# One-core recommender kernel: the last four single transfers become two paired ones, and the end pieces wait for less

## The chip, the cores and the metric

The kernel runs on one core of a Trainium2 chip. The metric is the device time of one execution in microseconds (us). Three runs of the kernel before the change took 133.70, 133.76 and 133.83 us; the median is 133.76 us.

## The reference, cut to what matters

The input is a matrix of 1024 rows (the batch) by 12500 columns in 32-bit floats, about 51 MB, and everything else is small. What is computed:

```python
x_reg = input_data @ W_lin.T + b_lin                       # 12500 -> 1
emb = input_data @ factors                                 # 12500 -> 16
sum_squared = jnp.square(emb.sum(axis=1))
squared_sum = (jnp.square(input_data) @ jnp.square(factors)).sum(axis=1)
h = jax.nn.relu(emb @ W1.T + b1)                           # 16 -> 128
h = jax.nn.relu(h @ W2.T + b2)                             # 128 -> 64
x = x_reg + 0.5 * (sum_squared - squared_sum)[:, None] + h @ W3.T + b3
x = 0.5 + jax.nn.sigmoid(x) * 5.0
```

Every element of the input is used twice by TensorE: once as it is (against 17 columns: the 16 factors and the linear weight) and once squared.

## The kernel before, in words

The input comes transposed, so that the 12500 dimensions lie on the partitions in chunks of 128. A first chunk and a remainder of 84 dimensions are loaded for all 1024 batch columns. The other 96 chunks are worked on in groups of eight (`CHUNKS`), each group for one half (512 columns) of the batch, so a group is 128 partitions x 8 x 512 floats, 2 MB, with 16 KB for each partition. Groups 0 to 11 are the first batch half. Groups 12 to 19 are the first 64 chunks of the second half (`TOTAL` is 20). The last 32 chunks of the second half, the end, come in nine smaller `PIECES`: four of the block of 352 columns, five of the block of 160.

All loads are issued from one queue, SyncE's (L263 to L290), in program order. The buffer `xr` has six slots of one group each. A load into a slot waits on the semaphore `sq_used` until the group that used the slot last has been multiplied: TensorE raises `sq_used` by one behind the last matmul of a group's squares, starting from `RING` = 3, so a value of 3 + n says that n groups are done. Groups 0 to 15 (`PAIRED`) are loaded two at a time, by one transfer of 4 MB with 32 KB for each partition (L268 to L274). Groups 16 to 19 are loaded one at a time, by transfers of 2 MB with 16 KB for each partition (L275 to L278), each with a semaphore of its own. The end pieces lie in slots 2 to 5 of `xr`, and piece i waits for `sq_used` to reach `RING + TOTAL - SLOTS + END_SLOT + last_slot(i) + 1` (L283), where `END_SLOT` is 2 and `last_slot(i)` is 0 to 3 for slots 2 to 5. In numbers: pieces 0 and 1 wait until group 17 is done, pieces 2 and 3 until group 18 is done, pieces 4 to 8 until group 19 is done.

What each engine does with a group: VectorE squares three of its eight chunks (L424 to L428), ScalarE squares five (L324 to L328), GpSimd copies its weights to a ring of three (`place`, L304 to L309), and TensorE multiplies the eight chunks (`multiply`) and then the eight squared chunks (`add_squares`), with 16 matmul instructions each. The eight chunks go to the four 32-column quarters of the array in turn. For a pair (`pair`) TensorE's order is: wait for the pair's landing, multiply both groups, then the squares of both. For a single group it is: wait for the group's landing, multiply it, then its squares. The squares go to a ring of three groups in `sq`.

Behind group 11 the dense layers of batch block 0 run (from 76 to 81 us in the profile). The end has an order written out by hand on TensorE, VectorE and ScalarE: `multiply_end(i)` and its squares for pieces 0 to 3, then pieces 4 to 8 mixed with the dense layers of block 1, and then the dense layers of block 2 (`first_layer`, `layer2`, `layer3`, a sigmoid and a scaling), the store and the end. The squares of pieces 0 to 3 are written over the `sq` ring, and for this `square_end` of piece 0 also waits until group 18 has been multiplied, and that of piece 2 until group 19 has.

Of the kernel before, what the change touches and what calls it, by code (L numbers as in the profile page):

```python
# [14 lines left out]
P = 128  # L15
# [4 lines left out]

REST = N % P
HALF = B // 2
CHUNKS = 8
# [5 lines left out]
GROUPS = (ALL - 1) // CHUNKS  # L32
END_GROUPS = ENDS // CHUNKS
TOTAL = 2 * GROUPS - END_GROUPS
PAIRED = 16
W_END = ALL - ENDS

END_SLOT = TOTAL % SLOTS
# [10 lines left out]

PITCH = CHUNKS * HALF + 64
PAIR_PITCH = TWO * CHUNKS * HALF + 64


# [27 lines left out]
HD = HD_L + REST_SETS * LIN  # L83


def fm_kernel(nc, head, x_first, x_rest, x_pairs, x_groups, x_end, out):
    with ExitStack() as ctx:
        def sb(name, shape, dt=F32):
            return ctx.enter_context(nc.sbuf_tensor(name, shape, dt))
# [4 lines left out]
        def sem(name):  # L94
            return ctx.enter_context(nc.semaphore(name))
# [38 lines left out]
        first_landed = sem("first_landed")  # L134
        rest_landed = sem("rest_landed")
        x_landed = [sem(f"x_landed{t}") for t in range(SLOTS // TWO)]
        single_landed = [sem(f"single_landed{g}") for g in range(PAIRED, TOTAL)]
        end_landed = [sem(f"end_landed{i}") for i in range(len(PIECES))]
        y_stored = sem("y_stored")
        zero_set = sem("zero_set")  # L140
# [91 lines left out]

            engine.wait_ge(x_landed[s // TWO], 16 * (r + 1))

        def single(engine, g):
            engine.wait_ge(single_landed[g - PAIRED], 16)

        def chunks(i):
            return sum(PIECES[i][2]) + sum(PIECES[i][3])

        def last_slot(i):
            k, c = PIECES[i][:2]
            return (ENDS * (BLOCKS[k][0] - HALF) + (c + chunks(i)) * BLOCKS[k][1] - 1) // (CHUNKS * HALF)
# [19 lines left out]
        @block.sync  # L263
        def _(sp):
            sp.dma_start(hd[:, :], head).then_inc(hd_landed, 16)  # L265
            sp.dma_start(xf[:, :], x_first).then_inc(first_landed, 16)  # L266
            sp.dma_start(xl[:, :, :].rearrange("p c b -> p (c b)"), x_rest).then_inc(rest_landed, 16)  # L267
            for p in range(PAIRED // TWO):  # L268
                at = TWO * p % SLOTS
                if TWO * p >= SLOTS:  # L270

                    sp.wait_ge(sq_used, RING + TWO * p + TWO - SLOTS)
                sp.dma_start(xr[:, at:at + TWO].rearrange("p s c b -> p (s c b)"),  # L273
                             x_pairs[p, :, 0:TWO * CHUNKS * HALF]).then_inc(x_landed[at // TWO], 16)  # L274
            for g in range(PAIRED, TOTAL):  # L275
                sp.wait_ge(sq_used, RING + g + 1 - SLOTS)
                sp.dma_start(xr[:, g % SLOTS].rearrange("p c b -> p (c b)"),
                             x_groups[g - PAIRED, :, 0:CHUNKS * HALF]).then_inc(single_landed[g - PAIRED], 16)  # L278
            at = 0
            for i in range(len(PIECES)):  # L280
                c, n = PIECES[i][1], chunks(i)
                rows = x_end[at:at + P * n * width(i)].rearrange("(p m) -> p m", p=P)
                sp.wait_ge(sq_used, RING + TOTAL - SLOTS + END_SLOT + last_slot(i) + 1)  # L283
                sp.dma_start(piece(i, c, n), rows).then_inc(end_landed[i], 16)
                at += P * n * width(i)

            for k in range(len(BLOCKS)):
                sp.wait_ge(y_ready[k], 1)
                sp.dma_start(out[cols(k)].rearrange("(q b) -> q b", q=4), y[0:P:32, line(k)]).then_inc(y_stored, 16)
            sp.wait_ge(y_stored, 16 * len(BLOCKS))  # L290
# [26 lines left out]
        @block.scalar  # L317
        def _(act):
            act.wait_ge(zero_set, 1)
            nc.scalar.activation(warm[:, :], zero[:, 0:1], ACT.Sigmoid)  # L320
            act.wait_ge(first_landed, 16)
            nc.scalar.activation(sqf[:, :], xf[:, :], ACT.Square).then_inc(first_squared, 1)  # L322

            def squares(r, s):  # L324

                act.wait_ge(sq_used, SLOTS * r + s + 1)
                nc.scalar.activation(sq[:, ring(s), BY_DVE:CHUNKS, :], xr[:, s, BY_DVE:CHUNKS, :],  # L327
                                     ACT.Square).then_inc(act_squared, 1)  # L328

            def square_end(i, j=0):  # L330
                c = PIECES[i][1] + sum(PIECES[i][2][:j])
                n = PIECES[i][2][j]
                if j == 0:
                    act.wait_ge(end_landed[i], 16)
                    if frees_more(i):
                        act.wait_ge(sq_used, squares_free(i))
                nc.scalar.activation(squared_piece(i, c, n), piece(i, c, n),  # L337
                                     ACT.Square).then_inc(act_end_squared, 1)

            def copy_lin(k, u):  # L340
                nc.scalar.copy(lin[:, part(k, u)], p_lin[k][:, u * BLOCKS[k][1] // 2:(u + 1) * BLOCKS[k][1] // 2]  # L341
                               ).then_inc(lin_ready[k], 1)

            def layer1(k, n):
                act.wait_ge(p_h1_done[k], 1)
                c = BLOCKS[k][0]
                nc.scalar.activation(h1[:, c:c + n], p_h1[0][:, 0:n], ACT.Relu,
                                     bias=pr[:, C_B1:C_B1 + 1]).then_inc(h1a_ready[k], 1)

            def embedding_square(k):  # L350
                act.wait_ge(p_es_done[k], 1)
                nc.scalar.activation(gsq[:, line(k)], tot_bank(k)[:, line(k)], ACT.Square).then_inc(gsq_ready[k], 1)

            def sigmoid(k):
                act.wait_ge(p_tot_done[k], 1)
                nc.scalar.activation(sg[:, line(k)], tot_bank(k)[:, line(k)], ACT.Sigmoid,
                                     bias=bias[:, :]).then_inc(sg_ready[k], 1)

            with act.Fori(0, GROUPS // SLOTS) as r:
                for s in range(SLOTS):  # L360
                    landed(act, r, s)
                    squares(r, s)

            act.wait_ge(sq_used, RING + GROUPS)
            copy_lin(0, 0)
            copy_lin(0, 1)
            layer1(0, BLOCKS[0][1] // 2)
            embedding_square(0)
            act.wait_ge(bias_ready, 1)
            sigmoid(0)  # L370

            for g in range(GROUPS, PAIRED):
                landed(act, g // SLOTS, g % SLOTS)
                squares(g // SLOTS, g % SLOTS)
            for g in range(PAIRED, TOTAL):
                single(act, g)
                squares(g // SLOTS, g % SLOTS)

            square_end(0, 0)
            square_end(0, 1)  # L380
            square_end(1, 0)
            square_end(1, 1)
            square_end(2)
            square_end(3)
            square_end(4, 0)
            act.wait_ge(p_lin_done[1], 1)
            copy_lin(1, 0)
            copy_lin(1, 1)
            nc.scalar.copy(rest[:, :], p_lin[1][:, BLOCKS[1][1]:HALF]).then_inc(rest_copied, 1)
            embedding_square(1)  # L390
            square_end(4, 1)
            layer1(1, BLOCKS[1][1])
            square_end(5, 0)
            square_end(5, 1)
            square_end(6, 0)
            square_end(6, 1)
            square_end(7, 0)
            square_end(7, 1)
            square_end(8)
            sigmoid(1)  # L400
            embedding_square(2)
            act.wait_ge(squares_done, 1)
            nc.scalar.copy(qs[:, :], p_sq[:, 0:BLOCKS[LAST][1]]).then_inc(qs_ready, 1)
            sigmoid(2)

        @block.vector
        def _(dve):
# [16 lines left out]
            def squares(r, s):  # L424

                dve.wait_ge(sq_used, SLOTS * r + s + 1)
                nc.vector.tensor_tensor(sq[:, ring(s), 0:BY_DVE, :], xr[:, s, 0:BY_DVE, :], xr[:, s, 0:BY_DVE, :],  # L427
                                        ALU.mult).then_inc(dve_squared, 1)  # L428
# [40 lines left out]
            layer2(0)  # L469
            scale(0)  # L470

            for g in range(GROUPS, PAIRED):
                landed(dve, g // SLOTS, g % SLOTS)
                squares(g // SLOTS, g % SLOTS)
            for g in range(PAIRED, TOTAL):
                single(dve, g)
                squares(g // SLOTS, g % SLOTS)

            square_end(0, 0)
# [24 lines left out]
        def _(pe):  # L504
# [40 lines left out]
            def multiply(r, s, h):  # L545
                pe.wait_ge(wr_ready, SLOTS * r + s + 1)
                for c in range(CHUNKS):
                    add_mm(quad(p_lin[h], c, LIN, 0, HALF), wr[:, ring(s), c, :], xr[:, s, c, :])
# [108 lines left out]
            embedding_square(0)  # L657
            layer3(0)

            for g in range(GROUPS, PAIRED, TWO):  # L660
                pair(g // SLOTS, g % SLOTS, 1)
            for g in range(PAIRED, TOTAL):
                single(pe, g)
                multiply(g // SLOTS, g % SLOTS, 1)
                add_squares(g // SLOTS, g % SLOTS, 1)

            pe.wait_ge(ws_ready, 2)
            for i in range(3):
# [102 lines left out]
```

## Time and profile before

| | |
|---|---|
| median of 3 runs | 133.76 us |
| the profiled execution | 133.76 us |
| its span in the profile | 132.0 us |
| mean granted TensorE clock | 0.974 |
| TensorE busy (matmul) | 107.0 us, 81% of the span |
| ScalarE, VectorE, GpSimd busy | 61.5, 52.6, 15.7 us |
| loaded from HBM | 52.2 MB, 396 GB/s over the span |

The span is the stretch from the first to the last record of the profile; 1.76 us of the execution's time lie around it. The chip's queues of transfers are busy nearly throughout. PE is TensorE, PEld its weight loads, SPq the queue of SyncE, which does nothing here but issue transfers. A granted clock of 1.00 is 2.4 GHz, one of 0.50 is 1.2 GHz.

### The profile page before, as it was taken

The numbers are of one execution on the slowest core, as the hardware profiler recorded it, in microseconds if no ns is written. First come the engines' busy times: TensorE is split into PE (matmuls) and PEld (weight loads), VectorE is DVE, ScalarE is ACT, GpSimd is POOL, SyncE is SP. The second block draws the span as 40 slices with busy tenths as digits, with TensorE's granted clock in tenths as the row PEclk, the third lists the DMA queues.
The fourth block names the chain that finished last, engine by engine and source line by source line (L and its number), as shares of the span: only waits on it lengthen the run. The fifth ranks groups of instructions, "written<-read, shape, count | busy, mean of one in ns | idle before, by whom it ended". The sixth has DMA issues, their size and how long they took to land.

```text
span 132.0 us, 2607 instructions
## 1 busy us (share of the span) xinstructions
PE 107.0 (81%) x1123; PEld 34.6 (26%) x1123; DVE 52.6 (40%) x51; ACT 61.5 (47%) x52; POOL 15.7 (12%) x48
## 2 busy tenths in 40 slices
PE   6099969429979839749749979999998987989992
PEld 4012222002212112112112233322222112345881
DVE  0391063027036036046045016565351351576571
ACT  4030067029039039049048046868562561465851
POOL 3015000200010200200200110164530000000000
PEclk9999999995999999999977999999999999999999
DMA  3999899989999998998999999899999999999700
GB/s 106 413 531 417 377 477 472 407 387 467 427 387 462 457 427 387 457 437 387 467 457 427 387 457 447 377 432 412 452 407 407 462 415 417 418 404 411 302 26 1
DMA packets 3489, 52.36 MB, mean 397 GB/s; under 512 B 404, under 2 KB 536, under 8 KB 1560
## 3 DMA queue, kind: packets, MB, share of 16 engines
q1 hardware_dynamic: 3480, 52.23, 93.2%
q8 instruction: 7, 0.11, 0.4%
q14 instruction: 2, 0.02, 0.0%
HBM read 52.22 MB, written 0.00 MB: 396 GB/s over the span
## 4 chain that ended last, share of the span: by engine, by line
DMA 54%; PE 40%; SPq 2%; DVE 1%; issue 1%; ACT 1%
DMA xr<-in_x_pairs 43%; PE p_lin L506 34%; DMA xr<-in_x_end 11%; PE p_sq L506 2%; PE p_h L601 2%; SPq L273 1%; PE p_tot L506 1%; PE p_h L632 1%; PE p_tot L614 0%; DVE h L454 0%; DVE h L449 0%; SPq L267 0%; SPq L266 0%; PE p_tot L621 0%; SPq L265 0%
## 5 line engine op out<-in xcount | busy, mean ns | idle before, releaser
L327 ACT ACTIVATE sq<-xr 128x2560 f32<-128x2560 f32 x20 | 45.9, 2333 | 46.8 <-DMA xr<-in_x_pairs 38.8
L427 DVE TENSOR_TENSOR sq<-xr 128x1536 f32<-128x1536 f32 x20 | 34.6, 1761 | 53.7 <-DMA xr<-in_x_pairs 42.9
L506 PE MATMUL p_lin<-xr,wr 128*17 128x512 f32 x320 | 39.9, 638 | 15.6 <-DMA xr<-in_x_pairs 14.4
L506 PE MATMUL p_lin<-sq,wz 128*18 128x512 f32 x320 | 37.7, 592 | 0.0
L506 PEld LDWEIGHTS p_lin<-xr,wr 128*17 128x17 f32 x320 | 9.2, 102 | 44.5 <-issue 38.4
L307 POOL COPY wr<-hd 128x136 f32 (+1 forms) x20 | 9.3, 464 | 75.0 <-PE p_lin L506 75.0
L506 PEld LDWEIGHTS p_lin<-sq,wz 128*18 128x18 f32 x320 | 10.1, 98 | 25.8 <-issue 25.0
L506 PE MATMUL p_lin<-xr,hd 128*17 128x352 f32 (+1 forms) x128 | 10.0, 380 | 1.3 <-DMA xr<-in_x_end 1.3
L437 DVE TENSOR_TENSOR sq<-xr 128x1408 f32<-128x1408 f32 (+3 forms) x6 | 6.6, 1135 | 6.1 <-DMA xr<-in_x_end 6.1
L337 ACT ACTIVATE sq<-xr 128x1408 f32<-128x1408 f32 (+3 forms) x6 | 5.7, 983 | 6.3 <-DMA xr<-in_x_end 6.3
L506 PE MATMUL p_lin<-sq,ws 128*18 128x352 f32 x64 | 6.6, 459 | 0.0
L506 PE MATMUL p_lin<-xf,hd 128*17 128x512 f32 x4 | 3.6, 1046 | 3.4 <-DMA xf<-in_x_first 3.4
L506 PEld LDWEIGHTS p_lin<-xr,hd 128*17 128x17 f32 x128 | 4.3, 97 | 5.2 <-issue 3.3
L308 POOL COPY wz<-s_all 128x8 f32 (+1 forms) x20 | 5.5, 273 | 0.0
L437 DVE TENSOR_TENSOR xr<-xr 128x320 f32<-128x320 f32 (+1 forms) x9 | 3.7, 451 | 2.2 <-DMA xr<-in_x_end 2.1
L506 PE MATMUL p_sq<-xr,ws 128*18 128x160 f32 x64 | 4.0, 300 | 0.0
L337 ACT ACTIVATE xr<-xr 128x320 f32<-128x320 f32 (+1 forms) x9 | 3.4, 432 | 0.9 <-DMA xr<-in_x_end 0.8
L449 DVE TENSOR_SCALAR h<-p_h,hd 128x256 f32<-128x256 f32 (+1 forms) x2 | 0.9, 434 | 6.9 <-PE p_h L601 6.8
L410 DVE SCALAR_TENSOR_TENSOR fsq<-hd 128x1552 f32<-128x1552 f32 x1 | 1.8, 1774 | 4.4 <-DMA hd<-in_head 4.4
L322 ACT ACTIVATE sqf<-xf 128x1024 f32<-128x1024 f32 x1 | 1.1, 1057 | 4.6 <-DMA xf<-in_x_first 4.6
L341 ACT COPY lin<-p_lin 128x256 f32<-128x256 f32 (+1 forms) x4 | 1.2, 342 | 4.2 <-PE p_lin L506 4.1
L506 PEld LDWEIGHTS p_lin<-sq,ws 128*18 128x18 f32 x64 | 2.4, 97 | 2.4 <-issue 1.4
(52 smaller groups left out, 40.8 us busy)
## 6 DMA issues: line engine op xcount, KB each, us to landing
xr<-in_x_pairs SPq DMA_DIRECT2D x8, 4096.0 KB, 21.9
xr<-in_x_groups SPq DMA_DIRECT2D x4, 2048.0 KB, 18.3
xr<-in_x_end SPq DMA_DIRECT2D x1, 2112.0 KB, 10.5
xr<-in_x_end SPq DMA_DIRECT2D x3, 640.0 KB, 12.0
xr<-in_x_end SPq DMA_DIRECT2D x1, 1760.0 KB, 14.3
xr<-in_x_end SPq DMA_DIRECT2D x1, 1056.0 KB, 12.4
hd<-in_head SPq DMA_DIRECT2D x1, 952.0 KB, 4.8
xr<-in_x_end SPq DMA_DIRECT2D x1, 704.0 KB, 13.7
```

Source lines behind the costliest of these rows:

```text
L273: sp.dma_start(xr[:, at:at + TWO].rearrange("p s c b -> p (s c b)"), x_pairs[p, :, 0:TWO * CHUNKS * HALF]).then_inc(x_landed[at // TWO], 16)
L307: nc.gpsimd.tensor_copy(wr[:, ring(s), :, :], w[:, bass.ds(at, CHUNKS), :]).then_inc(wr_ready, 1)
L308: nc.gpsimd.tensor_copy(wz[:, ring(s), :, LIN:WZ].rearrange("p c k -> p (c k)"), s_all[:, bass.ds(at, CHUNKS)]).then_inc(wz_ready, 1)
L327: nc.scalar.activation(sq[:, ring(s), BY_DVE:CHUNKS, :], xr[:, s, BY_DVE:CHUNKS, :], ACT.Square).then_inc(act_squared, 1)
L337: nc.scalar.activation(squared_piece(i, c, n), piece(i, c, n), ACT.Square).then_inc(act_end_squared, 1)
L341: nc.scalar.copy(lin[:, part(k, u)], p_lin[k][:, u * BLOCKS[k][1] // 2:(u + 1) * BLOCKS[k][1] // 2]).then_inc(lin_ready[k], 1)
L410: nc.vector.scalar_tensor_tensor(fsq[:, :, :], w[:, :, 0:EMB], -0.5, w[:, :, 0:EMB], ALU.mult, ALU.mult).then_inc(fsq_ready, 1)
L427: nc.vector.tensor_tensor(sq[:, ring(s), 0:BY_DVE, :], xr[:, s, 0:BY_DVE, :], xr[:, s, 0:BY_DVE, :], ALU.mult).then_inc(dve_squared, 1)
L437: nc.vector.tensor_tensor(squared_piece(i, c, n), piece(i, c, n), piece(i, c, n), ALU.mult).then_inc(dve_end_squared, 1)
L506: return nc.tensor.matmul(out, lhsT, rhs, start=False, stop=False, skip_group_check=True)
L601: mm = nc.tensor.matmul(bank[32 * t:32 * t + 32, 0:n], pr[:, C_W1 + 32 * t:C_W1 + 32 * t + 32], rhs, start=True, stop=True, skip_group_che ...
L632: mm = nc.tensor.matmul(p_h2[32 * t:32 * t + 32, row(k)], pr[:, C_W2 + t % 2 * 32:C_W2 + t % 2 * 32 + 32], h1[:, part(k, t // 2)], start=T ...
```

## The change

All twenty groups are loaded in pairs, so that the last four come by two transfers of 4 MB with 32 KB for each partition. `PAIRED`, the tensor `x_groups`, the semaphores `single_landed` and the loops over singles on SyncE, ScalarE, VectorE and TensorE go. Groups 16 and 17 go into slots 4 and 5 when group 11 is done, groups 18 and 19 into slots 0 and 1 when group 13 is done. TensorE works on them with `pair`. And `END_SLOT` goes out of the condition of the end pieces, which therefore wait for two groups less: pieces 0 and 1 until group 15 is done, pieces 2 and 3 until group 16 is, pieces 4 to 8 until group 17 is.

```diff
-            for p in range(PAIRED // TWO):
+            for p in range(TOTAL // TWO):
                 at = TWO * p % SLOTS
                 if TWO * p >= SLOTS:
                     sp.wait_ge(sq_used, RING + TWO * p + TWO - SLOTS)
                 sp.dma_start(xr[:, at:at + TWO].rearrange("p s c b -> p (s c b)"),
                              x_pairs[p, :, 0:TWO * CHUNKS * HALF]).then_inc(x_landed[at // TWO], 16)
-            for g in range(PAIRED, TOTAL):
-                sp.wait_ge(sq_used, RING + g + 1 - SLOTS)
-                sp.dma_start(xr[:, g % SLOTS].rearrange("p c b -> p (c b)"),
-                             x_groups[g - PAIRED, :, 0:CHUNKS * HALF]).then_inc(single_landed[g - PAIRED], 16)
...
-                sp.wait_ge(sq_used, RING + TOTAL - SLOTS + END_SLOT + last_slot(i) + 1)
+                sp.wait_ge(sq_used, RING + TOTAL - SLOTS + last_slot(i) + 1)
...
-            for g in range(GROUPS, PAIRED):
+            for g in range(GROUPS, TOTAL):
                 landed(act, g // SLOTS, g % SLOTS)
                 squares(g // SLOTS, g % SLOTS)
-            for g in range(PAIRED, TOTAL):
-                single(act, g)
-                squares(g // SLOTS, g % SLOTS)
...
-            for g in range(GROUPS, PAIRED, TWO):
+            for g in range(GROUPS, TOTAL, TWO):
                 pair(g // SLOTS, g % SLOTS, 1)
-            for g in range(PAIRED, TOTAL):
-                single(pe, g)
-                multiply(g // SLOTS, g % SLOTS, 1)
-                add_squares(g // SLOTS, g % SLOTS, 1)
```

VectorE's loops change as ScalarE's do. On the host, the rows of groups 16 to 19 are laid out as those of the other pairs.

## Rows read from the trace of the kernel before

**Rows 1.** Page, slices of the span, and the chain that ended last.

```profile
DMA  3999899989999998998999999899999999999700
...
DMA 54%; PE 40%; SPq 2%; DVE 1%; issue 1%; ACT 1%
```

**Rows 2.** Chain in order of time: start us, us, what.

```profile
38.47 7.10 PE p_lin L506 x64
...
67.65 8.66 PE p_lin L506 x64
...
80.17 20.91 PE p_lin L506 x192
101.08 0.02 issue
101.09 0.33 SPq L284
101.42 0.04 issue
101.47 14.35 DMA xr<-in_x_end
115.82 0.04 issue
115.86 6.75 PE p_lin L506 x92
```

**Rows 3.** Timeline of ScalarE, squares of pairs and singles: start, us, [idle before <-releaser].

```profile
28.74 4.57 ACT L327 ACTIVATE sq<-xr 128x2560 f32<-128x2560 f32 x2 [6.62 <-DMA xr<-in_x_pairs]
...
86.98 4.57 ACT L327 ACTIVATE sq<-xr 128x2560 f32<-128x2560 f32 x2 [1.87 <-DMA xr<-in_x_pairs]
91.88 2.35 ACT L327 ACTIVATE sq<-xr 128x2560 f32<-128x2560 f32 x1 [0.33 <-DMA xr<-in_x_groups]
...
106.56 2.35 ACT L327 ACTIVATE sq<-xr 128x2560 f32<-128x2560 f32 x1 [2.55 <-DMA xr<-in_x_groups]
111.61 1.38 ACT L337 ACTIVATE sq<-xr 128x1408 f32<-128x1408 f32 x1 [2.71 <-DMA xr<-in_x_end]
```

**Rows 4.** Stages of the end: us, busy of PE, PEld, DVE, ACT, POOL, PEclk, DMA share, GB/s.

```profile
106.56:111.61 5.05, 4.27 (x32) 0.92 (x32) 1.76 (x1) 2.35 (x1) 0.00 (x0) 1.00 1.00 427
115.84:121.79 5.95, 5.93 (x81) 2.96 (x85) 4.30 (x5) 3.73 (x5) 0.00 (x0) 1.00 1.00 408
121.79:127.04 5.25, 5.25 (x158) 4.46 (x155) 3.55 (x10) 4.61 (x14) 0.00 (x0) 1.00 0.57 223
```

**Rows 5.** Timeline, weight loads of TensorE that show its pace, groups and end pieces.

```profile
81.27 0.12 PEld L506 LDWEIGHTS p_lin<-xr,wr 128*17 128x17 f32 x4 [0.31 <-issue]
81.70 0.12 PEld L506 LDWEIGHTS p_lin<-xr,wr 128*17 128x17 f32 x4 [0.31 <-issue]
...
112.02 0.13 PEld L506 LDWEIGHTS p_lin<-xr,hd 128*17 128x17 f32 x4 [0.17 <-issue]
112.32 0.13 PEld L506 LDWEIGHTS p_lin<-xr,hd 128*17 128x17 f32 x4 [0.16 <-issue]
```

**Rows 6.** Timeline of TensorE: after pairs; the last group; the end pieces.

```profile
57.94 1.05 PE L506 MATMUL p_lin<-xr,wr 128*17 128x512 f32 x8 [2.67 <-DMA xr<-in_x_pairs]
...
106.58 1.91 PE L506 MATMUL p_lin<-xr,wr 128*17 128x512 f32 x16 [0.63 <-DMA xr<-in_x_groups]
...
111.73 0.49 PE L506 MATMUL p_lin<-xr,hd 128*17 128x352 f32 x4 [0.87 <-DMA xr<-in_x_end]
...
115.86 1.66 PE L506 MATMUL p_lin<-xr,hd 128*17 128x352 f32 x18 [0.39 <-DMA xr<-in_x_end]
```

**Rows 7.** Timeline around the landings of pieces 4 and 6.

```profile
121.72 0.17 PEld L506 LDWEIGHTS p_lin<-xr,hd 128*17 128x17 f32 x6 [0.17 <-DMA xr<-in_x_end]
...
124.93 0.49 DVE L437 TENSOR_TENSOR xr<-xr 128x320 f32<-128x320 f32 x1 [0.74 <-DMA xr<-in_x_end]
124.94 0.55 PEld L506 LDWEIGHTS p_lin<-xr,hd 128*17 128x17 f32 x16
124.98 0.30 PE L506 MATMUL p_sq<-xr,ws 128*18 128x160 f32 x2
125.03 0.80 PE L506 MATMUL p_lin<-xr,hd 128*17 128x160 f32 x16
```

**Rows 8.** Granted clock by stretches of 2 us, columns as in rows 4.

```profile
68.00:70.00 2.00, 2.00 (x12) 0.35 (x8) 2.00 (x2) 2.00 (x2) 0.00 (x0) 0.50 0.80 344
```

More of the change, by code:

```diff
@@ L34 @@
 TOTAL = 2 * GROUPS - END_GROUPS
-PAIRED = 16
 W_END = ALL - ENDS
@@ L48 @@
 BY_DVE = 3
-PITCH = CHUNKS * HALF + 64
 PAIR_PITCH = TWO * CHUNKS * HALF + 64
@@ L83, with fm_kernel @@
 HD = HD_L + REST_SETS * LIN
-def fm_kernel(nc, head, x_first, x_rest, x_pairs, x_groups, x_end, out):
+def fm_kernel(nc, head, x_first, x_rest, x_pairs, x_end, out):
     with ExitStack() as ctx:
@@ L136, in fm_kernel @@
         x_landed = [sem(f"x_landed{t}") for t in range(SLOTS // TWO)]
-        single_landed = [sem(f"single_landed{g}") for g in range(PAIRED, TOTAL)]
         end_landed = [sem(f"end_landed{i}") for i in range(len(PIECES))]
@@ L233, in landed @@
             engine.wait_ge(x_landed[s // TWO], 16 * (r + 1))
-        def single(engine, g):
-            engine.wait_ge(single_landed[g - PAIRED], 16)
         def chunks(i):
@@ L470, in _ @@
             scale(0)
-            for g in range(GROUPS, PAIRED):
+            for g in range(GROUPS, TOTAL):
                 landed(dve, g // SLOTS, g % SLOTS)
-                squares(g // SLOTS, g % SLOTS)
-            for g in range(PAIRED, TOTAL):
-                single(dve, g)
                 squares(g // SLOTS, g % SLOTS)
@@ L658, in _ @@
             layer3(0)
-            for g in range(GROUPS, PAIRED, TWO):
+            for g in range(GROUPS, TOTAL, TWO):
                 pair(g // SLOTS, g % SLOTS, 1)
-            for g in range(PAIRED, TOTAL):
-                single(pe, g)
-                multiply(g // SLOTS, g % SLOTS, 1)
-                add_squares(g // SLOTS, g % SLOTS, 1)
             pe.wait_ge(ws_ready, 2)
@@ L729 @@
     chunks = xT[P + REST:].reshape(ALL - 1, P, B)
-    x_pairs = np.zeros((PAIRED // TWO, P, PAIR_PITCH), f32)
-    x_groups = np.zeros((TOTAL - PAIRED, P, PITCH), f32)
+    x_pairs = np.zeros((TOTAL // TWO, P, PAIR_PITCH), f32)
     for g in range(TOTAL):
         h, c = g // GROUPS, CHUNKS * (g % GROUPS)
-        rows = chunks[c:c + CHUNKS, :, h * HALF:(h + 1) * HALF].transpose(1, 0, 2).reshape(P, -1)
-        if g < PAIRED:
-            at = g % TWO * CHUNKS * HALF
-            x_pairs[g // TWO, :, at:at + CHUNKS * HALF] = rows
-        else:
-            x_groups[g - PAIRED, :, :CHUNKS * HALF] = rows
+        at = g % TWO * CHUNKS * HALF
+        x_pairs[g // TWO, :, at:at + CHUNKS * HALF] = chunks[c:c + CHUNKS, :, h * HALF:(h + 1) * HALF].transpose(1, 0, 2).reshape(P, -1)
     ends = chunks[ALL - 1 - ENDS:]
@@ L762 @@
     params[:, C_B3] = np.asarray(L0_rec_b3)
-    arrays = {"head": head, "x_first": x_first, "x_rest": x_rest, "x_pairs": x_pairs, "x_groups": x_groups, "x_end": x_end}
+    arrays = {"head": head, "x_first": x_first, "x_rest": x_rest, "x_pairs": x_pairs, "x_end": x_end}
     nc = bacc.Bacc("TRN2", target_bir_lowering=False, num_devices=1)
```

## The prediction

> **What bounds the kernel now.** I read the page's slices first, then the chain in order of time, then the starts of ScalarE's squares, then the end in stages. The slices show transfers busy at 8 or 9 tenths up to the last two microseconds of the load, and the chain gives them 54% of the span [rows 1]. So for the first hundred microseconds the stream of loads is the bound: a pair lands, the engines work it off, and they wait. From the landing at 28.74 us to that at 86.98 us six pairs arrive, so one takes 58.24/6 = 9.71 us [rows 3]. The four singles take from 86.98 to 106.56 us, 19.58 us, or 4.895 each [rows 3]. The first question is whether the stream has a hole that earlier issues could close. It has none: the last group lands at 106.56, the first end piece at 111.61, and between the two the transfers are busy at a share of 1.00 with 427 GB/s [rows 3, 4], though that piece was issued only at 101.09 [rows 2]. It was issued late, yet 5.5 us before the queue would have run dry (106.56 - 101.09).
>
> The end has another bound. The chain's last step that waits for a transfer ends at 115.82, with piece 1, and behind it stand matmuls [rows 2]. From 115.84 to 121.79 TensorE is busy for 5.93 of 5.95 us, and from there to 127.04, when the last block's first sums are read, for 5.25 of 5.25 [rows 4]. Busy time alone could be drawn-out waiting, so I check it by pace. A group's weight loads come four at a time every 0.43 us (81.27, 81.70), those of an end piece of 352 columns every 0.295 us (112.02 and 112.32 give 0.30; I use 0.295) [rows 5]. Pieces 1, 2 and 3 have 10 + 6 + 4 = 20 chunks, each with two matmuls as it is and two squared: 80, or 20 steps of 0.295 = 5.9 us. From 115.86 this ends at 121.76, and piece 4, which lands near 121.7, is waited for with 0.17 us of idle weight loading and no more [rows 7]. So TensorE works without a pause from piece 1 on, and the loads arrive just in time. The Trainium skill (Trainium Kernel Development and Optimization, Performance Expectations) warns that matmul busy time is a bad metric, since matmuls are pipelined. That rule speaks against reading the 5.93 us as a bound; the pace of the weight loads agrees with it being one in this stretch.
>
> **The change part by part.** *Issue conditions of the end pieces.* They fall by two groups. Pieces 0 and 1 are then issued near 94 us in place of 101.09. I cost this at nothing: what hides it is the 5.5 us of transfers still ahead of them in the queue. Were that cover gone in the changed kernel, it would be a loss, but the issue is earlier, never later, and the pair of groups 18 and 19 waits for group 13, as group 19 does now. Below nothing the bound is that the pieces would arrive at the pair's pace of 432 GB/s (4.19 MB in 9.71 us) in place of 408 [rows 3, 4] for their 8.4 MB, some 1.1 us on the stream. I take zero: the share is already 1.00, and TensorE isn't waiting for that stream anyway.
>
> *Rows of 32 KB.* Two pairs take 19.42 us in place of the 19.58 of four singles [rows 3]. The last pair lands at 86.98 + 19.42 = 106.40, so the stream is 0.16 us ahead. Its bounds are 0 (if the 0.16 is the scatter of the landings) and 0.16; I take 0.16. Two issues on SyncE go, which lie beside the transfers.
> The Trainium skill (DMA: Bandwidth & Descriptors, the anatomy of one DMA) gives each transfer a fixed 2.0 us beside its bytes; it is measured on another issue path. By that rule alone two transfers fewer would give back 4 us. The singles' spacing of 4.895 us for 2.10 MB, against 6.8 by the rule, disagrees: in a full queue the fixed part lies beside the previous transfer [rows 3].
>
> *Groups 18 and 19 arrive together.* This is the part that costs. Now group 18 lands one group ahead of 19 and is worked off in the meantime, and only group 19's work is left behind the last landing of a group at 106.56. With the pair, two groups' work lies behind it. A group is 32 matmuls, eight steps of 0.43 = 3.44 us [rows 5]; the pair is 6.88. (A pair at the full clock takes 7.10 in the chain, with the run-out of its last matmul [rows 2].) The squares don't hold it up: the second group's ScalarE squares are ready 4.57 us behind the landing [rows 3], and TensorE wants them after 3 x 1.72 + 0.65 = 5.8 us. Then comes piece 0: 12 chunks, 48 matmuls, 12 steps of 0.295 = 3.54 us. Its squares may begin once group 18 is done, 5.2 us plus run-out behind the landing, near 111.9; they take ScalarE and VectorE some 2.4 us and are wanted at 115.1, so they are hidden.
> TensorE starts the pair at 106.42, ends it at 113.30, ends piece 0 at 116.84, and only then comes to piece 1, which it now starts at 115.86 [rows 6]. That is 0.98 us later. The other way round: today TensorE sits idle for 0.87 us before piece 0 and 0.39 before piece 1 [rows 6], plus some 1.1 us of waiting for squares and run-outs inside 106.58 to 115.86 (9.28 us less 3.44, 3.54, 0.87 and 0.39 leaves 1.04), 2.30 in all; group 18 puts 3.44 in, 0.16 come back from the stream: 3.44 - 2.30 - 0.16 = 0.98.
>
> *What of this reaches the end.* From piece 1 on TensorE has no pause that could take it up, except the short waits for pieces 4 and 6: under 0.1 us each, 0.13 together as I read them (121.72 against 121.79, 124.93 against 124.98) [rows 7]. The dense layers of block 1 and 2, the squares and the copies hang on TensorE's steps in the same order and move with it. So 0.98 - 0.13 = +0.85 us. In the profiled execution 133.76 becomes 134.61; that execution is equal to the median of the runs, 133.76, and so the forecast for the median is 134.6. If the stream gains nothing it is 134.77; if the pauses are larger than I read them (0.4 together) it is 134.3. The likeliest case's own range is 134.3 to 134.9.
>
> **The rivals.** *The clock falls before the last pair.* Between pairs TensorE sits idle for some 2.7 us (2.67 before the pair at 57.94, and so before the two new ones) [rows 6]; between singles it was idle for 0.63 at the last [rows 6]. After one of the three such pauses (before 48.2, 57.9 and 67.65 us) the granted clock was 0.50, that is 1.2 GHz, for the stretch from 68 to 70 us, and that pair took 8.66 us in place of 7.10 [rows 2, 8]. There it cost nothing, since the next pair was later. Before the last pair it adds up to 8.66 - 7.10 = 1.56 to the end: 134.6 + 1.56 = 136.2. For it: one of three. Against: the pause before the last pair is short if the pair before it was the slow one, and one of three is over other pauses. I give 0.13.
> The Trainium skill (TensorE: Matmul & The Clock Gate, HAM oscillation) describes such bursts between waits for transfers as falling back to half the clock each time; the three pauses here agree only in one.
>
> *TensorE's backlog is absorbed and the stream sets the end.* Then only the 0.16 us counts, and the time is 133.6, no change that can be told. For it: the chain gives transfers 54%, and the page's TensorE is at 81%. Against: the stages from 115.84 [rows 4]. It would decide from the point at which TensorE waits a full microsecond for pieces 2 to 8, taken together. Chance 0.07.
>
> *Faster: the end pieces arrive sooner.* If the 408 GB/s of the end is a matter of short queues and not of the pieces' shorter rows, queueing them near 94 us lets the stream run at 432 there and gains up to 1.1 us on the landings. It pays only if TensorE's work from 106.4 to 127 shrinks too, which it doesn't, or if its pace is held down by the transfers; it would decide from the point at which TensorE pauses for over a microsecond behind piece 1. I price it at -0.5 us, 133.2. Chance 0.04.
>
> *The change doesn't do what it says:* the 32 KB rows may be cut up so that the pace stays at 4.895 us a group. That is the 134.77 above, inside the forecast.
>
> **How the numbers follow.** Forecast 0.76, clock 0.13, stream 0.07, faster 0.04. A difference under 0.2% (0.27 us) can't be told from none. Slower: the first two, 0.89; same: 0.07; faster: 0.04. The forecast's own range leaves out 0.24 of the cases. I widen it upward to 135.6, which takes in half of the clock case (when part of the pair is under the low clock, or the median of runs falls between), and downward to 133.9 for pauses in TensorE's end that I haven't seen.
>
> **What would show it.** Right: ScalarE's squares of the last pair start near 106.4, one wait and not two; TensorE works without a pause from there to 127.9; piece 1's multiplications start near 116.8 though it lands near 115.7; the wait for piece 4 is gone; and TensorE is idle for some 2.7 us before 96.7 and before 106.4. Wrong: idle time of TensorE between 106.4 and 127, a landing of piece 1 far from 115.7, or an end that hasn't moved though piece 1 starts a microsecond late. The clock rival shows as a granted clock of 0.50 behind 106.4.

## The result: 134.72 us, 0.66% slower

The changed kernel took 134.65 to 134.81 us in four runs, median 134.72; the kernel before, on the same chip, 133.70 to 133.97, median 133.80. The ratio is 1.0066 (95% interval 1.0054 to 1.0079). Six more executions in a later session gave 134.58 to 134.78, ratio 1.0061 (1.0044 to 1.0077). The forecast was 134.6. The profiled execution took 134.81 us with a span of 132.9. Here and below, medians and ranges take in every execution, while the ratios leave out slow ones (one of 136.75 us and one of 137.56 us, in two of the experiments) and are not the ratio of the medians where the times scatter.

The page after the change, busy time and chain. TensorE and the transfers do the same work in a longer span (1123 matmul records and 52.23 MB in both). The chain now goes along the pairs, up to 106.40 us, and from there along matmuls.

```profile
span 132.9 us, 2603 instructions
PE 104.7 (79%) x1123; PEld 33.4 (25%) x1123; DVE 52.5 (39%) x51; ACT 61.1 (46%) x52; POOL 13.8 (10%) x48
DMA 58%; PE 35%; SPq 2%; DVE 1%; issue 1%; ACT 1%
```

The chain in order of time, which answers to [rows 2]: before, the last step that waited for a transfer ended at 115.82, with piece 1. Now it ends at 106.40, with the last pair.

```profile
78.62 6.91 PE p_lin L489 x64
85.53 0.02 issue
85.55 20.85 DMA xr<-in_x_pairs
106.40 0.04 issue
106.45 17.08 PE p_lin L489 x208
```

ScalarE's squares, which answer to [rows 3]. The last pair starts at 106.42, in one wait; the end pieces land at or before 111.9, at 115.69 and at 118.24.

```profile
86.99 4.57 ACT L316 ACTIVATE sq<-xr 128x2560 f32<-128x2560 f32 x2 [3.42 <-DMA xr<-in_x_pairs]
96.70 4.57 ACT L316 ACTIVATE sq<-xr 128x2560 f32<-128x2560 f32 x2 [5.14 <-DMA xr<-in_x_pairs]
106.42 4.57 ACT L316 ACTIVATE sq<-xr 128x2560 f32<-128x2560 f32 x2 [5.15 <-DMA xr<-in_x_pairs]
111.92 2.06 ACT L326 ACTIVATE sq<-xr 128x1408 f32<-128x1408 f32 x2 [0.93 <-PE p_lin L489]
115.69 1.77 ACT L326 ACTIVATE sq<-xr 128x1408 f32<-128x1408 f32 x2 [1.70 <-DMA xr<-in_x_end]
118.24 1.08 ACT L326 ACTIVATE sq<-xr 128x1056 f32<-128x1056 f32 x1 [0.79 <-DMA xr<-in_x_end]
```

TensorE, which answers to [rows 6]. The two pauses before pieces 0 and 1 (0.87 and 0.39 us) are gone; the matmuls run through, and piece 1, which landed at 115.69, is started at 116.88 in place of 115.86.

```profile
106.45 3.63 PE L489 MATMUL p_lin<-xr,wr 128*17 128x512 f32 x32 [2.66 <-DMA xr<-in_x_pairs]
109.89 3.62 PE L489 MATMUL p_lin<-sq,wz 128*18 128x512 f32 x32
113.33 1.96 PE L489 MATMUL p_lin<-xr,hd 128*17 128x352 f32 x24
115.10 1.96 PE L489 MATMUL p_lin<-sq,ws 128*18 128x352 f32 x24
116.88 1.65 PE L489 MATMUL p_lin<-xr,hd 128*17 128x352 f32 x18
...
122.79 0.74 PE L489 MATMUL p_lin<-xr,hd 128*17 128x160 f32 x16
```

The last scaling on VectorE before the store, first of the kernel before, then of the changed one: it is 0.97 us later, and the span ends 0.9 us later.

```profile
129.82 0.18 DVE L459 TENSOR_SCALAR y<-sg 128x40 f32<-128x40 f32 x1 [0.70 <-ACT sg L356]
```

```profile
130.79 0.18 DVE L445 TENSOR_SCALAR y<-sg 128x40 f32<-128x40 f32 x1 [0.70 <-ACT sg L345]
```

### The profile page after: what moved, and what is told of

It reads as the page before. It is cut to its first block, busy times and chain, and to the rows that moved or that the text cites. A ratio compares the mean times of both kernels' runs of the same rounds, so it can differ in the third digit from the quotient of the medians.

```text
span 132.9 us, 2603 instructions
## 1 busy us (share of the span) xinstructions
PE 104.7 (79%) x1123; PEld 33.4 (25%) x1123; DVE 52.5 (39%) x51; ACT 61.1 (46%) x52; POOL 13.8 (10%) x48
## 3 DMA queue, kind: packets, MB, share of 16 engines
q1 hardware_dynamic: 3192, 52.23, 92.5%
## 4 chain that ended last, share of the span: by engine, by line
DMA 58%; PE 35%; SPq 2%; DVE 1%; issue 1%; ACT 1%
DMA xr<-in_x_pairs 58%; PE p_lin L489 30%; PE p_sq L489 2%; PE p_h L584 2%; SPq L266 1%; PE p_tot L489 1%; PE p_h L615 1%; PE p_tot L597 0%; DVE h L435 0%; DVE h L440 0%; SPq L260 0%; SPq L259 0%; PE p_tot L604 0%; SPq L258 0%; ACT lin L330 0%
## 5 line engine op out<-in xcount | busy, mean ns | idle before, releaser
L489 PE MATMUL p_lin<-sq,wz 128*18 128x512 f32 x320 | 36.2, 592 | 0.0
L296 POOL COPY wr<-hd 128x136 f32 (+1 forms) x20 | 7.4, 372 | 80.6 <-PE p_lin L489 80.6
L489 PEld LDWEIGHTS p_lin<-sq,wz 128*18 128x18 f32 x320 | 9.5, 98 | 24.8 <-issue 24.8
L584 PE MATMUL p_h<-lin,hd 128*32 128x256 f32 (+2 forms) x32 | 2.5, 386 | 0.5 <-ACT lin L330 0.5
```

Of the source, the lines that this page charges most:

```text
L296: nc.gpsimd.tensor_copy(wr[:, ring(s), :, :], w[:, bass.ds(at, CHUNKS), :]).then_inc(wr_ready, 1)
L489: return nc.tensor.matmul(out, lhsT, rhs, start=False, stop=False, skip_group_check=True)
L584: mm = nc.tensor.matmul(bank[32 * t:32 * t + 32, 0:n], pr[:, C_W1 + 32 * t:C_W1 + 32 * t + 32], rhs, start=True, stop=True, skip_group_che ...
```

## The experiments

Three questions: is it TensorE's backlog behind the last pair; which part of the change does it; and what does the clock do in the pauses between pairs. Each kernel was executed 5 to 12 times, beside the kernel before.

**Is it the backlog? Taking work away.** In the changed kernel, of group 18's squares only the last chunk is multiplied:

```diff
-            def add_squares(r, s, h):
+            def add_squares(r, s, h, few=False):
...
-                for c in range(BY_DVE):
+                for c in range(0 if few else BY_DVE):
...
-                for c in range(BY_DVE, CHUNKS):
+                for c in range(CHUNKS - 1 if few else BY_DVE, CHUNKS):
...
-                pair(g // SLOTS, g % SLOTS, 1)
+                landed(pe, g // SLOTS, g % SLOTS)
+                multiply(g // SLOTS, g % SLOTS, 1)
+                multiply(g // SLOTS, g % SLOTS + 1, 1)
+                add_squares(g // SLOTS, g % SLOTS, 1, g in (18,))
+                add_squares(g // SLOTS, g % SLOTS + 1, 1, g + 1 in (18,))
```

> The changed kernel without 14 of the 16 square matmuls of group 18 (its output lacks them): 1.5 us of TensorE's work less behind the last pair, and nothing else changed. Theory: TensorE would be at piece 1 by 115.4 and waits for its landing at 115.7, so the end goes by the stream, which is 0.16 us ahead of the kernel before: 133.6 us, ratio 0.998 to 0.9995; the gain is 1.1 us and not 1.5. Rival (the loss comes from the transfers or from elsewhere): the time stays at 134.7.

Measured: 133.88 us at the median of 11, against 133.80 before, ratio 1.0023 (1.0000 to 1.0047); nine of the eleven took 133.69 to 134.00 and two 135.13 and 135.20. In these nine the loss is gone with the work, though nothing was changed in the transfers. The stream's lead of 0.16 us didn't come out as a gain: piece 4 is started 0.27 us sooner than before the change (121.52), but the copy of the last block's sums only 0.06 us sooner (126.98 against 127.04). What takes up the rest in between isn't settled. The two executions at 135.1 were not profiled.

**The same from the other side: adding work to the kernel before.** Matmuls of zeros between group 19's squares and piece 0, eight and then twelve of them:

```diff
+            for _ in range(8):
+                add_mm(p_sq[:, 0:HALF], zero[:, 0:P], zero[:, 0:HALF])
             pe.wait_ge(ws_ready, 2)
```

> The kernel before with 8 matmuls of zeros (bf16, 512 columns, about 0.215 us each at 2.4 GHz, 1.72 us) put between group 19's squares and piece 0 on TensorE. Theory: between 106.6 and 115.86 TensorE has about 1.7 us of pauses that such work can fill (2.30 in all, 0.6 of them a wait inside group 19 for ScalarE's squares), so the time hardly moves: 133.8 to 133.9 us, ratio 1.000 to 1.001. Rival (TensorE is the bound all the way, or its busy time in this stretch is real): +1.7 us, ratio 1.013.

> As the run with 8 matmuls of zeros, with 12 of them, 2.58 us. Theory: the pauses take up 1.7 us, and what is over, 0.9 us, reaches the end in full: 134.7 us, ratio 1.006 to 1.007, as much as the change costs. Rival (the end has further slack behind piece 1): under 1.003.

Measured: 134.01 us with eight, ratio 1.0017 (1.0008 to 1.0026), and 134.86 with twelve, ratio 1.0084 (1.0071 to 1.0097), against 133.80. Eight cost 0.21 us for 1.72 of work; the next four cost 0.85 for 0.86 of work. So the pauses take up about 1.5 us, a little less than the 1.7 that I expected, and of the work beyond them the whole reaches the end. In the profile with twelve, TensorE stands as in the changed kernel: piece 1 starts at 117.01, with no pause before it.

```profile
110.75 2.76 PE L506 MATMUL p_sq<-zero 128*128 128x512 bf16 x12
113.45 1.97 PE L506 MATMUL p_lin<-xr,hd 128*17 128x352 f32 x24
115.23 1.96 PE L506 MATMUL p_lin<-sq,ws 128*18 128x352 f32 x24
117.01 1.65 PE L506 MATMUL p_lin<-xr,hd 128*17 128x352 f32 x18
```

**Which part? The issue condition alone.** The kernel before with singles, `END_SLOT` taken out of L283:

> The kernel before, with only the end pieces' condition relaxed by two groups; groups 16 to 19 stay singles. Theory: the stream had no hole, so the time stays at 133.8 us, ratio 0.999 to 1.001, and the pieces land within 0.1 us of where they did (111.61, 115.84). Rival (early issues lift the end's 408 to 427 GB/s towards the pairs' 432): the pieces land up to 0.5 us sooner, and since TensorE waits for piece 4 the time falls by up to 0.5 us, ratio 0.996.

Measured: 133.85 us against 133.87, ratio 0.9999 (0.9990 to 1.0008). The pieces are issued from 94.23 on in place of 101.09, and pieces 0 and 1 land at 111.57 and 115.78, within 0.06 us of before. With singles the condition is worth nothing.

**The pairs alone.** The changed kernel with the old condition:

```diff
-                sp.wait_ge(sq_used, RING + TOTAL - SLOTS + last_slot(i) + 1)
+                sp.wait_ge(sq_used, RING + TOTAL - SLOTS + END_SLOT + last_slot(i) + 1)
```

> The changed kernel with the end pieces' old condition: all groups in pairs, but piece i waits for two groups more again. Theory (the cost is TensorE's backlog behind the last pair): the issue condition is worth nothing, so this takes the changed kernel's time, 134.7 us, ratio to before 1.006 to 1.008; piece 1 lands near 115.7 and is started near 116.9. Rival (the early issues cost something, by mixing with the last pair's packets): about 133.7, ratio 0.999.

Neither theory held. The six executions took 134.76, 136.69, 136.76, 135.49, 136.56 and 136.64 us; ratio 1.0193 (1.0166 to 1.0221). Only the one that was profiled, 134.76, is where I expected them all. It shows what I had left out. The first pieces are issued at 103.75, when group 17 is done and 2.6 us before the last pair has landed (106.31), and yet the stream thins out. The same stretches of the changed kernel, and then of this one, with columns as in [rows 4] (the last three are clock, share of the transfer engines and GB/s):

```profile
103.50:105.00 1.50, 0.29 (x4) 0.00 (x0) 0.00 (x0) 0.00 (x0) 0.00 (x0) 1.00 0.86 357
105.00:106.30 1.30, 0.00 (x0) 0.00 (x0) 0.00 (x0) 0.00 (x0) 0.00 (x0) 1.00 0.88 377
```

```profile
103.50:105.00 1.50, 0.19 (x4) 0.00 (x0) 0.00 (x0) 0.00 (x0) 0.00 (x0) 1.00 0.71 189
105.00:106.30 1.30, 0.00 (x0) 0.00 (x0) 0.00 (x0) 0.00 (x0) 0.00 (x0) 1.00 0.49 169
```

189 and 169 GB/s in place of 357 and 377 over 2.8 us leave some 0.52 MB undone, 1.2 us of the stream, and piece 2 lands at 119.38 in place of 118.24. In this execution TensorE's backlog hides it: TensorE comes to piece 7, which lands near 127.05, at 127.07, without a pause.

**One pair only, groups 16 and 17.** `PAIRED = 18` in the kernel before:

> The kernel before with PAIRED = 18: groups 16 and 17 come as a pair, 18 and 19 stay singles, the end's condition is the old one. Theory: a pair costs nothing where TensorE has time behind it, and group 19 alone lies behind the last landing; the rows of 32 KB put the stream 0.08 us ahead: 133.7 us, ratio 0.999 to 1.000. Rival (any pair delays work that is missed later): part of the 0.9 us shows here, ratio 1.002 to 1.004.

Measured: 134.61 to 136.75 us in six executions, median 136.48, ratio 1.0137 (1.0089 to 1.0186); both theories missed. The profiled execution, at 136.50, shows what happened. The clock fell as the pair arrived, its multiplications took 5.30 us in place of 3.63, and group 17 was done only at 105.5. The first pieces, which wait for it, were issued at 105.56, and the stream ran dry (columns as in [rows 4]; the clock is the third number from the end):

```profile
98.00:100.00 2.00, 2.00 (x12) 0.34 (x8) 2.00 (x2) 2.00 (x2) 0.00 (x0) 0.50 1.04 442
104.00:106.00 2.00, 2.00 (x24) 0.54 (x20) 0.00 (x0) 0.00 (x0) 0.31 (x2) 1.00 0.23 98
106.00:108.00 2.00, 2.00 (x24) 0.54 (x20) 1.50 (x1) 1.50 (x1) 0.00 (x0) 1.00 0.84 194
```

Piece 0 lands at 113.36 in place of 111.61, piece 1 at 117.58 in place of 115.84 and piece 2 at 121.10 in place of 118.40: 2.7 us, which is the loss at the end.

**The same pair with the early condition.** `PAIRED = 18`, and `END_SLOT` out of the condition:

> Groups 16 and 17 a pair, 18 and 19 singles, as in the run that took 134.6 to 136.75, but with the end pieces' condition relaxed by two groups. Theory formed from that run's profile: its 2 us came from the end pieces, issued only when the clock-slowed pair of 16 and 17 was done (105.56) and so leaving a hole in the stream; with the early condition they are issued near 94 and the hole is gone: all executions 133.6 to 134.2, ratio 0.999 to 1.002. Rival (the slow pair's work itself is what is late): still up to 136.7.

Measured: 133.73 us, twelve executions within 133.56 to 133.86, ratio 0.9990 (0.9981 to 0.9999). The theory held. This version is 1.0 us below the changed kernel and 0.1 us below the kernel before, a difference whose interval all but reaches 1. In its profile the pieces are issued from 94.22 on, and the last group alone stands behind the last landing of a group, with the pauses of 0.88 and 0.39 us before pieces 0 and 1 as before. That execution's clock was whole at the pair; that a fall there is harmless with the early condition is seen in the changed kernel itself, below.

**The last pair only.** Groups 16 and 17 as singles, 18 and 19 a pair, early condition:

> The changed kernel with groups 16 and 17 as singles again (rows of 16 KB out of the same tensor), 18 and 19 a pair, the end's condition relaxed. Theory: the whole cost is here, and it lacks half of the 0.16 us that the 32 KB rows gave the stream: 134.8 us, ratio 1.007 to 1.008; piece 1 is started near 116.95. Rival: the loss is split between the two pairs, ratio 1.003 to 1.005.

Measured: 136.26 to 137.61 us in five executions, median 136.57, ratio 1.0204 (1.0186 to 1.0222). The cost is 2.7 us, nearly three times what I expected, because I hadn't seen how long TensorE would now wait: 5.50 us, from the end of group 17 to the pair. In the profiled execution, which is the slowest (137.61), the clock falls in this pause (third number from the end in the first two lines), and the pair's multiplications take 6.41 us in place of 3.63:

```profile
104.00:106.00 2.00, 0.00 (x0) 0.00 (x0) 0.00 (x0) 0.00 (x0) 0.00 (x0) 0.84 1.07 454
106.00:108.00 2.00, 1.45 (x8) 0.33 (x12) 1.47 (x1) 1.47 (x1) 0.00 (x0) 0.50 1.01 431
...
106.55 6.41 PE L502 MATMUL p_lin<-xr,wr 128*17 128x512 f32 x32 [5.50 <-DMA xr<-in_x_pairs]
...
119.77 1.65 PE L502 MATMUL p_lin<-xr,hd 128*17 128x352 f32 x18
```

Piece 1 starts at 119.77, 2.9 us later than in the changed kernel. The other four, 136.26 to 137.00, weren't profiled. By estimate, the 134.8 expected and a slowed pair as in two other runs (5.30 us for 3.63) give 136.5, which fits them. How the cost would split between the two pairs at a whole clock this experiment doesn't show; that it lies with the last pair follows from the one before, where the pair of 16 and 17 costs nothing.

**A longer pause before the last pair.** The changed kernel with one chunk of squares in place of eight for groups 16 and 17, edited as in the first experiment with `(16, 17)` for `(18,)`:

> The changed kernel without 14 of the 16 square matmuls of each of groups 16 and 17 (its output lacks them), so that TensorE sits idle for some 5.7 us in place of 2.66 before the last pair; the work behind the last pair is whole. Theory of the clock rival: the granted clock falls to 0.50 before or at 106.4, the last pair takes up to 8.7 us in place of 6.9, and with no slack behind it the time is 136.2 us or somewhat over, ratio 1.015 to 1.020, although less is computed. Rival (the clock stays, or the end takes it up): 134.7.

Measured: 134.66 to 137.56 us in six executions, median 136.44, ratio 1.0156 (1.0114 to 1.0198). Less is computed, and it takes longer. The profiled execution, 136.55, has the fall twice, at pair 16 and 17 and again before the last pair, whose multiplications took 5.28 us. Its pause before the last pair was 2.99 us and not 5.7: the slowed pair before it took 1.4 us more (5.01 for 3.63), and its four matmuls of squares, all in one quarter of the array, went one every 0.43 us, 1.88 in all. So the longer pause was not reached here; it stands only in the kernel before this one, with 5.50 us.

**Does the changed kernel meet this?** It was run again, and with the pauses filled:

```diff
             for g in range(GROUPS, TOTAL, TWO):
+                if g >= 16:
+                    for _ in range(8):
+                        add_mm(p_sq[:, 0:HALF], zero[:, 0:P], zero[:, 0:HALF])
                 pair(g // SLOTS, g % SLOTS, 1)
```

> The changed kernel itself, unchanged, in more executions. What was measured so far: four executions within 134.65 to 134.81; without group 18's squares, 9 of 11 at 133.7 to 134.0 and 2 at 135.1 to 135.2. Clock theory: about two in ten executions have the clock fall just before the last pair and take 136.0 to 136.3, the others 134.6 to 134.9. Rival (the two at 135.1 belong to the left-out work): all within 134.6 to 134.9.

> The changed kernel with 8 matmuls of zeros (1.72 us at the full clock) on TensorE before it waits for each of the last two pairs, so that its pause there is about 1 us in place of 2.66. Clock theory: the clock can't fall there any more, every execution takes 134.6 to 134.9; the extra work costs nothing, since it ends before the landing. Rival (the pauses are not what brings the clock down): the spread of the changed kernel stays.

Measured: 134.58 to 134.78 for the kernel itself, six executions, and 134.64 to 134.74 with the pauses filled (median 134.70, ratio 1.0063). With the four of the first session, ten executions of the changed kernel show no 136. I expected two in ten; the rival's case was not met, and filling the pauses had nothing to mend. In the profile of the repeated run, at 134.78 us, though, the clock did fall at the pair of groups 16 and 17, and it cost nothing: the pieces had been issued since 94.15, TensorE only lost part of its next pause (1.01 us in place of 2.66), and piece 1 starts at 116.93.

```profile
96.73 5.33 PE L489 MATMUL p_lin<-xr,wr 128*17 128x512 f32 x32 [2.65 <-DMA xr<-in_x_pairs]
101.88 3.62 PE L489 MATMUL p_lin<-sq,wz 128*18 128x512 f32 x32
106.50 3.63 PE L489 MATMUL p_lin<-xr,wr 128*17 128x512 f32 x32 [1.01 <-DMA xr<-in_x_pairs]
...
116.93 1.65 PE L489 MATMUL p_lin<-xr,hd 128*17 128x352 f32 x18
```

The Trainium skill (TensorE: Matmul & The Clock Gate, HAM oscillation) tells of bursts between waits for transfers that each start at half the clock. The trace agrees only in part: the pause of 2.65 us before this pair was followed by multiplications at the lower clock here (5.33 us) and not in the first profile of the same kernel (3.63), and in the pause of 5.50 us the clock fell.

**The late condition with the pauses filled.** All pairs, old condition, and the matmuls of zeros:

> All groups in pairs with the end pieces' old condition, which took 134.76 once and 136.6 in most executions, now with the same 8 matmuls of zeros before each of the last two waits. Theory: the 136.6 needs a clock-slowed pair 16 and 17; with the pauses filled the pieces are issued at 103.6, the hole in the stream is 0.7 us and lies under TensorE's backlog: 134.7 to 135.0 in all executions. Rival (the late condition costs 2 us by itself): 136.6.

Measured: 135.02 to 136.18 us in six executions, median 135.34, ratio 1.0118 (1.0090 to 1.0145). Five are within 135.02 to 135.51, clear of the 136.6 that four of six took without the filling. That is in line with the theory that the 136.6 needs the slowed pair, but doesn't prove it: none of those four was profiled, and the slowed pair with the late condition was seen only in the kernel with one pair. What speaks for the place of a fall and not for their number is that the executions at 134.76 and at 136.69 have the same mean clock (0.972 and 0.974).

The 134.7 to 135.0 that I expected is missed, by 0.3 to 0.6 at the median. In the profile (135.39 us, whole clock from 62 us on) the first pieces are issued at 103.88 and piece 2 lands at 119.52, much as in the profiled execution without the filling (103.75, 119.38), which took 134.76; the landings of piece 7 are 127.19 and 127.05. What differs is piece 8, the last. One issue on SyncE took 1.49 us, where none took over 0.45 in the other profile, piece 8 was issued at 116.4 in place of 115.2, and TensorE waited half a microsecond for it:

```profile
114.91 1.49 SPq L273 DMA_DIRECT2D xr<-in_x_end  x1
...
128.10 0.10 PEld L489 LDWEIGHTS p_lin<-xr,hd 128*17 128x17 f32 x2 [0.50 <-DMA xr<-in_x_end]
```

The copy of the last block's sums is then at 128.67 in place of 128.04, 0.63 us later, and the time is 0.63 longer. I take it that with the late condition the last pieces are issued so close to their use that a slow issue shows; the profile has the two side by side and doesn't prove it. What the other five executions lose stays open.

## Why the prediction was right, point by point

*What bounds the end.* Right. TensorE has no pause from 106.45 to 128 us, and work added there moves the end one for one once the pauses are filled (0.85 us for 0.86).

*Rows of 32 KB: 0.16 us on the stream.* Right in the landings: 106.42 against 106.56, a lead of 0.14. A single profile scatters by about as much, but all of them together agree: from the landing near 87 us to that near 106.4 it takes 19.27 to 19.48 us in the seven profiles with two pairs there and 19.44 to 19.67 in the four with singles, 0.16 apart in the mean. As part of the time it isn't shown: the sum takes it off the end (TensorE starts the pair that much sooner), and no run separates it from the rest.

*Groups 18 and 19 together: +0.98 at piece 1.* Forecast 116.84, measured 116.88, +1.02 over 115.86. Pair and piece 0 came out at 6.88 and 3.55 us for the 6.88 and 3.54 of the sum.

*0.13 us taken up by the waits for pieces 4 and 6.* This term was too large. Piece 4 is started at 122.79 in place of 121.79, 1.00 later, so the wait there had given back 0.02; the last block's copy is 0.96 later (128.00 against 127.04) and the last scaling 0.97. The forecast of +0.85 for the profiled execution stands against +0.9 to +1.05 (132.9 against 132.0 in span, 134.81 against 133.76 in time), and +0.92 by the medians. Nearly all of the difference lies in this term.

*The end's condition: nothing.* Right for the kernel with singles (0.9999), but the cover I named, 5.5 us of queued transfers, is a property of the singles. With pairs and the old condition it was 2.6 us in the profiled execution (103.75 to 106.31) and 0.9 us where the clock had slowed the pair before (105.56 to 106.50, in the kernel with one pair), and this isn't enough: four of six executions lose another 1.9 us. So the condition is worth nothing by itself and a good deal in the changed kernel. I had written that without the cover there would be a loss, but gave it no size and didn't see that the pairs take the cover away. The sum came out since the change has both edits.

*The rivals.* The stream setting the end and the earlier pieces are out: the landings of pieces 1 and 2 moved by 0.15 us (115.84 to 115.69) and 0.16 us (118.40 to 118.24), and the last scaling by +0.97. The clock before the last pair was a real mechanism with a price near the one given (the made cases reach 136.0 to 137.6; I said 136.2), but it didn't occur in ten executions. Whether it can in this kernel is open: at the chance of 0.13 that I gave it, ten executions would be free of it once in four times. What I missed is the other place for a fall, at the pair before, where it acts through the issue of the end pieces.

## What to carry to other kernels

Where a stream of loads sets the pace, look at how much work stands behind the last large landing: merging the last transfers gained 0.8% of their time (19.41 us for 19.57 in the mean of the profiles) and put a whole group's work behind the point from which the compute engine has no pause left. Merge the early transfers, if at all, and keep the last ones single: merging one more early pair gained 0.1 us at most here. And when transfers are merged, move the issue conditions of those behind them as well: a condition tied to an engine's progress has a cover in microseconds of queued bytes, and that cover has to outlast that engine's slowest case, here a pair at half the clock.

## What the runs showed that I hadn't expected

The stream thins out well before a transfer of 4 MB has landed when the next ones are issued only 2.6 us before that: 189 and 169 GB/s in its last 2.8 us in place of 357 and 377, with a mean busy share of the transfer engines of 0.71 and 0.49. That lost 1.2 us of stream. Issued 0.9 us before the last group's landing, pieces 0 to 2 came 1.7 to 2.7 us late; issued 5.5 us before it (the kernel before), no later than when issued 12 us before.

The clock's falls look harmless in the kernel before. Its profile has two, at 1.2 GHz for some 3.4 us each (29.9 to 33.3 and 67.4 to 70.8 us), with a mean clock of 0.974; its other executions have 0.948 to 0.987, and their times lie within 133.6 to 134.4 us. With a pair of groups 16 and 17 and the late condition such a fall was seen to delay the pieces, and the times scatter by 2 us.
